# Layer 1 of a fused four-layer graph network: the order of its first and last steps on three engines, and two more half scalings on ScalarE

## Time and profile before

| | |
|---|---|
| median of 3 runs | 558.47 us (558.32 to 558.75) |
| the profiled execution | 557.26 us, span 555.5 us |
| TensorE (PE) busy | 523.4 us, 94% |
| TensorE weight load (PEld) | 472.0 us, 85% |
| VectorE (DVE) busy | 415.9 us, 75% |
| ScalarE (ACT) busy | 369.2 us, 66% |
| GpSimd (POOL) busy | 194.1 us, 35% |
| mean granted clock of TensorE | 0.991 |

### The profile page before, as it was taken

How to read it: one execution, slowest core, us unless ns; L and a number is a source line. 1 busy time by engine, 2 the same in 40 slices (tenths; PEclk the granted TensorE clock), 3 DMA queues, 4 the chain that set the end, 5 groups by cost and what they waited for, 6 DMA issues and landing times.

```text
span 555.5 us, 11182 instructions
## 1 busy us (share of the span) xinstructions
PE 523.4 (94%) x3684; PEld 472.0 (85%) x3684; DVE 415.9 (75%) x1465; ACT 369.2 (66%) x764; POOL 194.1 (35%) x237
## 2 busy tenths in 40 slices
PE   7999998799987799999999999999999999999963
PEld 6998635689986798988989999999998998989953
DVE  4899677987874543589787687788678676788797
ACT  4776793556864445364686785786787677676874
POOL 4970352355434314117027026116216215310203
PEclk9999999999999899999999999999999999999988
DMA  6631000346423110000000100100100100100002
GB/s 189 185 96 38 0 0 20 93 131 205 139 88 108 57 39 2 1 1 1 2 2 2 38 1 0 38 0 0 38 0 0 38 1 0 38 2 1 21 19 76
DMA packets 34180, 23.72 MB, mean 43 GB/s; under 512 B 2992, under 2 KB 32816, under 8 KB 34144
## 3 DMA queue, kind: packets, MB, share of 16 engines
q1 hardware_dynamic: 32144, 17.58, 10.6%
q0 software_dynamic: 1712, 5.44, 3.1%
q10 hardware_dynamic: 288, 0.26, 0.1%
HBM read 14.88 MB, written 8.39 MB: 42 GB/s over the span
## 4 chain that ended last, share of the span: by engine, by line
PE 79%; DVE 14%; ACT 2%; issue 2%; POOL 2%; POOLq 0%; DVEq 0%; ACTq 0%
PE psum L292 15%; PE psum L293 15%; PE psum L294 15%; PE psum L2172 10%; PE psum L1961 5%; PE psum L2019 3%; PE psum L2124 2%; PE psum L2114 2%; PE psum L2027 2%; PE psum L2218 2%; PE psum L2200 2%; PE psum L2036 1%; PE psum L1888 1%; DVE soft L1116 1%; PE psum L2192 1%
## 5 line engine op out<-in xcount | busy, mean ns | idle before, releaser
L208 POOL TENSOR_TENSOR ln_r<-ln_v,mhalf 128x8 f32<-128x8 f32 x25 | 41.1, 1642 | 216.2 <-DVE ln_v L202 216.2
L2172 PE MATMUL psum<-l2w_s,h 128*128 128x128 f32 x512 | 59.7, 275 | 0.0
L2172 PEld LDWEIGHTS psum<-l2w_s,h 128*128 128x128 f32 x512 | 59.0, 192 | 0.6
L292 PE MATMUL psum<-qt_hi,l2w_s_hi 128*128 128x512 f32 x128 | 52.7, 412 | 0.0
L293 PE MATMUL psum<-qt_lo,l2w_s_hi 128*128 128x512 f32 x128 | 50.6, 395 | 0.0
L294 PE MATMUL psum<-qt_hi,l2w_s_lo 128*128 128x512 f32 x128 | 50.6, 395 | 0.0
L286 ACT ACTIVATE keep_x<-keep_x,ln_b,ln_r (+1 forms) x104 | 42.7, 487 | 2.6 <-POOL ln_b L211 2.6
L1688 ACT ACTIVATE h<-psum 128x512 f32<-128x512 f32 x60 | 34.8, 593 | 11.7 <-PE psum L294 11.6
L292 PE MATMUL psum<-wgt_hi,h_hi 128*128 128x256 f32 x128 | 37.2, 291 | 1.1 <-DVE h_lo L1093 0.9
L293 PE MATMUL psum<-wgt_lo,h_hi 128*128 128x256 f32 x128 | 35.8, 280 | 0.0
L294 PE MATMUL psum<-wgt_hi,h_lo 128*128 128x256 f32 x128 | 35.7, 279 | 0.0
(11 more groups left out here) (297 smaller groups left out, 1745.0 us busy)
## 6 DMA issues: line engine op xcount, KB each, us to landing
keep_x<-in_x SPq DMA_DIRECT2D x32, 128.0 KB, 2.9
xin<-in_x SPq DMA_DIRECT2D x32, 128.0 KB, 2.3
v_rows<-vst SPq DMA_DIRECT2D x32, 128.0 KB, 2.1
out_x<-ob SPq DMA_DIRECT2D x24, 128.0 KB, 1.8
out_x<-keep_x SPq DMA_DIRECT2D x8, 128.0 KB, 2.0
l2w_raw<-in_l2w POOLq DMA_DIRECT2D x1, 512.0 KB, 5.0
adjs<-in_adj_t ACTq DMA_DIRECT2D x2, 128.0 KB, 2.6
adjs<-in_adj SPq DMA_DIRECT2D x2, 128.0 KB, 2.8
```

Source lines behind the costliest of these rows:

```text
L208: pool.tensor_tensor(ln.r[:].rearrange("p s k -> p (s k)"), ln.v[:].rearrange("p s k -> p (s k)"), mhalf[:], ALU.pow).then_inc(ln.root, 1)
L292: pe.matmul(o, lhs[0], rhs[0], start=start, stop=False)
L2172: i = pe.matmul(bank(s)[:, 0, k * D:(k + 1) * D], h2[:, s, g, j * N + t * P:j * N + (t + 1) * P], l2w3_s[:, g, :], start=(g == 0), stop=(g ...
```

## The change

1. Slots 2 and 3 get the treatment of slots 0 and 1: VectorE applies the norm to quarters 0 and 2 only, ScalarE scales quarters 1 and 3 (`first_scale`, behind `q_high(1)` and ahead of `v_copied(1)`). VectorE computes the negated mean and POOL the shift for them too; POOL's powers of slots 4 and 5 wait for these scalings as well, and `turn_x1(2)` and `(3)` wait for both signals.
2. VectorE's order at the start changes: `q_low(0)`, `q_low(1)`, the sums and the leaky steps move forward, and from pair 3 on both `q_low` of a pair stand ahead of `moments0`. At the end of the loop `q_low(13)` stands ahead of `take_attention(0)`.
3. TensorE, p = 6: `turn_attention(0)` moves behind the second projections and `score_slot(5, 1)`.
4. TensorE, last pair: `project(14, *)` moves ahead of `attend1(0, 0)`, `project(15, *)` ahead of `output1(0, 0)`.
5. ScalarE: `weighted_high(1, 0)` and `(1, 1)` move ahead of `z_copied(14)` and `(15)`. VectorE: `add(0, 1)` moves ahead of `weighted_low(1, 1)`.

```diff
--- before.py
+++ after.py
@@ -590,10 +590,10 @@
 
 
             for q in range(6):
-                if 2 <= q < 4:
+                if q >= 2:
 
                     pool.wait_ge(ln0_done[1], q - 1)
-                first_power(pool, q, ln0, q < 2)
+                first_power(pool, q, ln0, q < 4)
 
             def bn_out(p):
 
@@ -1001,30 +1001,30 @@
             sum0_slot(1, 0)
             first_apply(dve, 1, ln0, (0, 2), ln0_done[0], 1)
             first_stats(dve, 2, ln0)
-            first_moments(dve, 2, ln0, False)
+            first_moments(dve, 2, ln0, True)
             sum0_slot(1, 1)
+            q_low(0)
             first_stats(dve, 3, ln0)
-            first_apply(dve, 2, ln0, range(4), ln0_done[0], 2)
-            first_moments(dve, 3, ln0, False)
-            q_low(0)
+            first_moments(dve, 3, ln0, True)
+            first_apply(dve, 2, ln0, (0, 2), ln0_done[0], 1)
             sum0_slot(2, 0)
-            first_apply(dve, 3, ln0, range(4), ln0_done[1], 2)
+            q_low(1)
+            sum0_slot(2, 1)
+            first_apply(dve, 3, ln0, (0, 2), ln0_done[0], 1)
             first_stats(dve, 4, ln0)
             first_moments(dve, 4, ln0, False)
-            sum0_slot(2, 1)
-            q_low(1)
+            leaky_slot(0, 0)
             first_stats(dve, 5, ln0)
             first_apply(dve, 4, ln0, range(4), ln0_done[0], 2)
             first_moments(dve, 5, ln0, False)
-            leaky_slot(0, 0)
             sum0_slot(3, 0)
+            leaky_slot(0, 1)
             first_apply(dve, 5, ln0, range(4), ln0_done[1], 2)
-            leaky_slot(0, 1)
             sum0_slot(3, 1)
             stats0(3)
             q_low(2)
+            q_low(3)
             moments0(3)
-            q_low(3)
             for p in range(2, IT - 2):
                 leaky(p - 1)
                 if p == IT - 3:
@@ -1033,15 +1033,15 @@
                 apply0(p + 1)
                 stats0(p + 2)
                 q_low(2 * p)
+                q_low(2 * p + 1)
                 moments0(p + 2)
-                q_low(2 * p + 1)
             maxima(0)
             leaky(IT - 3)
             apply0(IT - 1)
             normalize(0)
             q_low(2 * (IT - 2))
+            q_low(2 * (IT - 2) + 1)
             take_attention(0)
-            q_low(2 * (IT - 2) + 1)
             leaky(IT - 2)
 
             def add(p, s, done, psum_bank, ln):
@@ -1073,8 +1073,8 @@
             first_moments(dve, 0, ln1, True)
             q_low(Q - 1)
             weighted_low(1, 0)
+            add(0, 1, o1_done, 6, ln1)
             weighted_low(1, 1)
-            add(0, 1, o1_done, 6, ln1)
             first_apply(dve, 0, ln1, (0, 2), ln1.done, 1)
             first_stats(dve, 1, ln1)
             first_moments(dve, 1, ln1, True)
@@ -1634,7 +1634,10 @@
             x1_turned(1)
             for s in range(2):
                 bn_out_slot(3, s, False)
-            projected(0, 1)
+            q_high(1)
+            for q in range(2, 4):
+                first_scale(act, q, ln0, (1, 3), ln0_done[1])
+            v_copied(1)
             edge_log()
             z_copied(0)
             for p in range(1, IT - 1):
@@ -1659,9 +1662,9 @@
                 projected(IT - 1, s)
                 y1_turned(0, s, 6 - 6 * s)
             for s in range(2):
+                weighted_high(1, s, False)
+            for s in range(2):
                 z_copied(Q - 2 + s)
-            for s in range(2):
-                weighted_high(1, s, False)
             for q in range(2):
                 first_scale(act, q, ln1, (1, 3), ln1.one_scaled)
                 xs_high(q)
@@ -1996,11 +1999,12 @@
 
             def turn_x1(q):
 
-                if q < 2:
+                if q < 4:
                     for s in range(2):
                         pe.wait_ge(ln0_done[s], q + 1)
                 else:
                     pe.wait_ge(ln0_done[q % 2], 2 * (q // 2) + 2)
+                if q >= 2:
                     pe.wait_ge(z_ready, q - 1)
                 for j in range(2):
                     for t in range(T):
@@ -2097,11 +2101,11 @@
                 score_slot(p - 1, 0)
                 for s in range(2):
                     project(2 * p + s, 0)
+                for s in range(2):
+                    project(2 * p + s, 1)
+                score_slot(p - 1, 1)
                 if p == IT - 2:
                     turn_attention(0)
-                for s in range(2):
-                    project(2 * p + s, 1)
-                score_slot(p - 1, 1)
                 for s in range(2):
                     select(2 * p + s)
 
@@ -2294,15 +2298,15 @@
 
             for s in range(2):
                 turn_x1(Q - 2 + s)
+            for k in range(2):
+                project(Q - 2, k)
             pe.wait_ge(sm, SM_STEPS)
             attend1(0, 0, 6)
             for k in range(2):
-                project(Q - 2, k)
+                project(Q - 1, k)
             pe.wait_ge(ln0.added, Q)
             output1(0, 0, 1)
             attend1(0, 1, 0)
-            for k in range(2):
-                project(Q - 1, k)
             score(IT - 2)
             output1(0, 1, 6)
             for s in range(2):
```

More of the change, by code:

```diff
@@ L2099, in _ @@
                     project(2 * p + s, 0)
-                if p == IT - 2:
-                    turn_attention(0)
                 for s in range(2):
@@ L2104, in _ @@
                 score_slot(p - 1, 1)
+                if p == IT - 2:
+                    turn_attention(0)
                 for s in range(2):
```

## The result

The changed kernel takes 548.91 us (548.45 to 549.37, 4 runs) against 558.59 us before (558.32 to 558.75, 4 runs): ratio 0.9827, 95% interval 0.981 to 0.9844, or 9.7 us less. The forecast was 549.6. Between the two profiled executions the difference is smaller, 557.26 to 549.37, 7.9 us, and so is that of the spans, 555.5 to 547.6.

A forecast was written before the change was run, and what follows sets the result against it. TensorE held 79% of the chain, layer 1 having a filled middle and two loose ends; start -0.7 and end -8.15 sum to -8.85 us, giving a median of 549.6 us (548.4 profiled), range 547.5 to 553.3.

The forecast's parts named there:

- (a): End of layer 1: second projections and score_slot(5,1) cover turn_attention(0)'s 1.2 us wait for the reciprocal chain, -1.35 us.
- (b): End of layer 1: project(14,*) and project(15,*) fill the waits ahead of attend1(0,0) and output1(0,0), -3.2 us.
- (c): End of layer 1: earlier high parts let add(0,1) start 8.75 us earlier; mix_x(0,1) gains 8.15, containing (a) and (b).
- The cover of 2.7 us for POOL's products: End of layer 1: POOL's products ready at 172.4, 2.7 us before ScalarE makes the high parts at about 175.1.
- rival 2: End of layer 1: late POOL products keep add(0,1) behind the selects; only the start, (a) and (b) pay: 553.2, chance 0.12.
- The start: Start of layer 1: VectorE's lighter, reordered queue brings project(4,0) from 123.40 to 122.7, -0.7 us, bounds -0.1 and -1.5.
- VectorE's column: Start of layer 1: VectorE's last sum of the first four pairs moves from 115.24 to 114.6, 0.6 us earlier.
- rival 3: Start of layer 1: a 2.3 us gap ahead of select(2) drops TensorE's clock, costing 1.6 us: 551.2, chance 0.13.
- The cover for the later moments: Loop, five turns: moments come 0.6 us later, but 1.2 us between POOL's shift and ScalarE's scaling leaves 0.6 spare.

The follow-up runs named there:

- end_pe_only: Kernel before plus only TensorE's moves at the end (turn_attention, project(14,*), project(15,*)) and q_low(13) ahead of take_attention: 553.05 us, ratio 0.9903.
- c_only: Kernel before plus only ScalarE's high parts ahead of z_copied(14), (15) and add(0,1) ahead of weighted_low(1,1): 554.48 us, ratio 0.9923.
- start_only: Kernel before plus only the start (ScalarE's two more halves, VectorE's new order up to and in the loop), old end: 558.6 us against 558.53, ratio 1.0002.
- bridged_short: Changed kernel plus 6 idle matmul calls on TensorE in the gap ahead of select(2): 547.68 us, ratio 0.9798.
- before_warm: Kernel before plus idle matmul calls (2, 4, 2 and 6) in TensorE's four waits at the end of layer 1: 557.48 us against 557.98, ratio 0.9999.
- end_only: Kernel before plus only the end of the change (TensorE's moves, q_low(13), high parts, add(0,1)), old start and loop: 548.68 us, ratio 0.9833.
- before_again: Kernel before, unchanged, run for a second trace: 557.89 us against 557.98, ratio 0.9998.
- bridged: Changed kernel plus 20 idle matmul calls on TensorE in the gap ahead of select(2): 552.77 us, ratio 0.9906.
- q_early: Changed kernel with VectorE's q_low(2) and q_low(3) moved ahead of the last sum and statistics of pair 3: 551.47 us, ratio 0.9871.

## Why the prediction was right, and where it was not

**The total** lies 0.7 from the forecast, but two errors of opposite sign are in it, so that it came so close is in part luck. In the profiled execution, for which the sum was made, the forecast was 548.4 and the measurement 549.37, 1.0 above it; the median came out 0.7 below.

**(a), (b), (c)** held step by step. At project(10,0) the changed kernel is 0.7 behind the one before, where the forecast had it 0.7 ahead; with that taken off: select(12) to turn_x1(14) gains 1.36 (forecast 1.35), select(14) 4.66 (4.55), add(0,1) 8.85 (8.75), mix_x(0,1) 8.39 (8.15). end_pe_only and c_only show each half at work by its own mechanism, and their medians add. The cover of 2.7 us for POOL's products held (rival 2 fell): ScalarE turned to them at 175.69 without waiting for POOL.

**The start** failed. VectorE's column was right: the last sum at 114.73 (114.6), the variance at 119.08 (119.0), the shift done at 121.34 (121.26). Within it, two sizes were off and cancelled. Slot 5's root took 1.01 and not 1.38, although leaky(0,1) ran beside it: it began 0.37 ahead of that step, while the roots of 1.38 and 1.31 began inside one. And apply5 took 1.88 beside POOL's bn_out (L604), 1.41 in the first trace of the kernel before. What failed is the step from the sum to TensorE: "the first is done at 122.7, and project(4,0), at 123.40 before, starts there". The 2.3 us gap that the text itself names under rival 3 was 2.7, and behind it the clock was at 0.50. Rival 3 occurred, at 1.5 us as priced (1.6), and belonged in the sum and not beside it. start_only puts the whole start at 0.0 in place of -0.7, bridged_short shows 1.1 to 1.2 of it as the clock's.

Behind that 0.0 stand two kinds of old start. With the old order the ruler of the start reads 23.70 in three traces (before, before_warm, end_only), in which apply5 took 1.41. In the three others apply5 took 1.87, q_low(2) came later and TensorE waited 0.8 us for it: 24.16 where the clock held (c_only), 25.72 and 25.78 where it fell (before_again, end_pe_only). The new order had 1.88 or 1.87 in all six traces, and it reads 24.09 and 24.08 where its gap is left open. So against the old start it loses 0.4 us in its quick executions and gains 1.6 in those where the clock fell. Why the same instructions take 1.41 or 1.87 stays open.

**The profiled execution** was the second error. The sum was made against 557.26 and moved to the median by adding 1.2 on both sides. But those 1.2 were not a constant: in the changed kernel the profiled execution lies 0.5 above the median. The other 1.3 belong to the kernel before, whose first trace was a quick one. Each execution has a mean granted clock, 0.991 for that trace; one fall like those in layer 1 takes some 0.003 off it (an estimate: 3.3 us at half clock, of 555.5). Of 59 later executions of the same kernel only two had 0.991, and took 557.03 and 557.16; 14 with 0.988 have a median of 557.5, 37 with 0.985 or 0.986 one of 558.5. So, by this estimate, a usual execution has one or two more falls than the trace the sum was made from, and they go with 1.3 us.

A mean does not tell where the falls lie. The traces show places: the old start (two of six traces), and the old waits near 171 to 176 in start_only and c_only (1.7 and 1.4 us). The new end has no wait over 1.1 left, and in all six traces with it the clock stayed at 1.00 from 157 to 185. That the falls it removes are what the medians show beyond the traces fits, and is not shown; nor is what put the changed kernel's profiled execution 0.5 above its median.

**The loop.** The cover for the later moments held; no wait of TensorE stands in it. A turn took 8.99 to 9.00 and not 8.93 in the changed kernel and in start_only, but 8.93 to 8.95 in both bridged kernels with the same order, so the order alone is not the cause. The 0.06 stay unexplained.

## What to carry to other kernels

A queue in program order makes work wait for copies it has no need of; look for an engine that idles before a step while the next step's input is complete, and price it by that gap. And a gap that is moved on TensorE must be priced with the clock behind it, by what stands there: here a fall cost 1.5 us ahead of selects, 2.5 ahead of 32 dense projections, and nothing at 187, where VectorE ended the path. So moving a gap ahead of denser work can lose. Take more than one trace of the kernel before where its executions spread, before a sum is built on one.

## What the runs showed of the hardware

- The granted clock fell with single waits of 2.1 us (q_early) and 2.7 us (changed kernel, start_only), not only of 3.1. With the same 2.0 us wait it fell in c_only (0.66 in 170 to 175) and, a little later, in start_only (0.83 there), and stayed at 1.00 in both traces of the kernel before.
- At the old start, whose longest wait is 1.3 us, it fell in two of six traces (0.64 in before_again, 0.57 in end_pe_only).
- Filled with idle matmuls, one gap kept the clock at 1.00 (bridged_short, 1.00 in 118 to 122). In before_warm four waits were filled and it fell at 193, behind a 1.0 us wait.
- One idle call of 256 float32 columns shows as two passes and takes 0.43 us (20 calls, 40 passes, 8.5 us in bridged).
- POOL's power of a slot took 1.31 or 1.38 us where it began inside a leaky or an xs_lo step of VectorE, both with two inputs in SBUF, and 1.01 to 1.04 otherwise.
- Four applies on VectorE took 1.10 to 1.12 us alone. Beside POOL's two scalings of 512 columns (L604) they took 1.41 in some executions, with POOL's pair at 2.51, and 1.87 or 1.88 in others, with POOL's pair at 1.82.
